# The next pair's value projection ahead of the last pair's final context group: a changed TensorE order in a two-layer attention kernel

## What is computed

```
q, k, v = tanh(x @ Wq + bq), tanh(x @ Wk + bk), tanh(x @ Wv + bv)     # per head: 1024 x 64
alpha   = softmax(causal(q @ k^T / sqrt(64)))
ctx     = alpha @ v
return tanh(ctx @ Wo + bo)
```

## Time and profile before

| | |
|---|---|
| median of 3 executions | 1946.13 us (1944.18 to 1951.32) |
| the profiled execution, its own time | 1945.94 us |
| its span in the trace | 1944.2 us |
| TensorE matmul busy | 1750.4 us, 90% |
| VectorE busy | 1436.0 us, 74% |
| ScalarE busy | 1376.0 us, 71% |
| GpSimd busy | 362.4 us, 19% |
| mean granted TensorE clock | 0.964 |

### The profile page before, as it was taken

One profiled execution on the slowest core, in us unless ns is written; L12 is line 12 of the kernel. 1 busy time (PEld: TensorE's weight loads), 2 busy tenths in 40 slices (PEclk: granted clock), 3 DMA queues, 4 the chain that ended last, 5 costly groups with the idle time before them and its releaser, 6 DMA issues. The chain is left out here.

```text
span 1944.2 us, 38151 instructions
## 1 busy us (share of the span) xinstructions
PE 1750.4 (90%) x12846; PEld 767.9 (39%) x12933; DVE 1436.0 (74%) x2573; ACT 1376.0 (71%) x1943; POOL 362.4 (19%) x349
## 2 busy tenths in 40 slices
PE   2899999999999999654999999999999999989995
PEld 2344444444444444330233333333333333256774
DVE  4477777888778888887677777777777777548888
ACT  4666666666666666352888888888888888855776
POOL 4111113333333333365200000000000000020004
PEclk8999999999999999866999999999999999989998
DMA  4101000000111000058011110111000100000001
GB/s 124 50 34 36 34 34 35 34 34 34 38 40 38 34 34 3 4 120 187 1 19 20 20 19 18 18 18 18 18 18 18 18 18 19 1 13 7 17 11 43
DMA packets 44966, 63.24 MB, mean 33 GB/s; under 512 B 7554, under 2 KB 32802, under 8 KB 43172
## 3 DMA queue, kind: packets, MB, share of 16 engines
q1 hardware_dynamic: 43856, 60.62, 11.6%
q10 hardware_dynamic: 1044, 1.76, 0.2%
HBM read 20.94 MB, written 13.11 MB: 18 GB/s over the span
## 5 line engine op out<-in xcount | busy, mean ns | idle before, releaser
L1348 ACT ACTIVATE arena<-psum 128x512 f32<-128x512 f32 x1024 | 556.3, 609 | 115.1 <-PE psum L1423 90.4
L630 ACT ACTIVATE arena<-psum 128x2048 f32<-128x2048 f32 (+1 forms) x160 | 273.3, 1708 | 231.6 <-PE psum L515 228.9
L1446 PE MATMUL psum<-arena 128*128 128x512 bf16 x983 | 302.4, 388 | 47.6 <-DVE arena L1054 22.2
L1054 DVE TENSOR_REDUCE arena<-psum 128x1 f32<-128x1024 f32 x256 | 309.7, 1210 | 28.8 <-PE psum L1446 27.7
L1049 DVE CUSTOM_DVE_ANT_0 arena<-psum,arena 128x512 f32<-128x512 f32 x256 | 177.0, 691 | 170.8 <-ACT arena L1340 170.1
L1423 PE MATMUL psum<-arena 128*128 128x512 bf16 x978 | 291.0, 382 | 10.1 <-ACT arena L1348 7.5
L532 PE MATMUL psum<-arena,hs 128*64 128x512 f32 (+3 forms) x1536 | 283.0, 496 | 2.7 <-POOL arena L679 2.2
L679 POOL TENSOR_SCALAR_AFFINE_SELECT arena<-arena 128x512 f32<-128x512 f32 (+1 forms) x160 | 168.9, 1073 | 563.5 <-ACT arena L630 563.5
L1436 PE MATMUL psum<-arena 128*32 128x512 f32 x2048 | 272.8, 605 | 0.7 <-ACT arena L1348 0.7
L515 PE MATMUL psum<-arena 64*128 64x512 f16 (+3 forms) x2304 | 215.4, 325 | 4.9 <-DVE arena L714 3.6
L1423 PEld LDWEIGHTS psum<-arena 128*128 128x128 bf16 x1024 | 98.4, 97 | 269.2 <-ACT arena L1348 193.9
(11 more groups left out here) (194 smaller groups left out, 2377.2 us busy)
## 6 DMA issues: line engine op xcount, KB each, us to landing
arena<-arena SPq DMA_DIRECT2D x32, 512.0 KB, 3.0
arena<-arena SPq DMA_DIRECT2D x48, 128.0 KB, 2.2
latent_k<-arena SPq DMA_DIRECT2D x12, 384.0 KB, 5.0
latent_kpm<-arena SPq DMA_DIRECT2D x12, 384.0 KB, 5.2
arena<-latent_q SPq DMA_DIRECT2D x48, 96.0 KB
arena<-latent_kpm SPq DMA_DIRECT2D x16, 288.0 KB
arena<-latent_k SPq DMA_DIRECT2D x16, 288.0 KB
arena<-arena SPq DMA_DIRECT2D x32, 96.0 KB, 2.6
```

Source lines behind the costliest of these rows:

```text
L630: nc.scalar.activation(probs[g], SC[:, :, 0:WIDTH[g]], ACT.Exp, scale=DH ** -0.5).then_inc(exp_done, 1)
L1054: nc.vector.tensor_reduce(tops[:, m:m + 1], slot, AX.X, ALU.max).then_inc(top_done, 1)
L1348: nc.scalar.activation(e_probs[u % 2][:, j, :], TS[(GH * u + j) % 3], ACT.Exp, scale=KD ** -0.5).then_inc(e_done, 1)
L1446: last = nc.tensor.matmul(slot[:, h * HALF:(h + 1) * HALF], q_rows[par][:, j, qt * P:(qt + 1) * P], k[:, j, h * HALF:(h + 1) * HALF], star ...
```

## The change

On TensorE alone, in each pair, the value projection of the next pair now stands ahead of the final context group of the last pair. Nothing else differs: the same instructions, the same waits, the same buffers.

```diff
@@ -563,10 +563,10 @@
                 def pair(i, par, last=False, norm=False):
+                    if not last:
+                        values(i + 1, 1 - par)
                     if at_least(i, 1):
                         context(i - 1, 4, 1 - par)
-                    if not last:
-                        values(i + 1, 1 - par)
                     scores(i, 1, par)
                     if not last:
                         project(i + 1, 0, 1 - par)
```

## The result

The changed kernel takes 2020.23 us (median of 4 executions, 1997.05 to 2026.54) against 1946.26 for the kernel before on the same chip, 74 us more. The recorded ratio is 1.0354, with a 95% interval of 1.027 to 1.0439; it isn't the quotient of the two medians, which is 1.038. I had forecast 1995 and a range that ended at 2003. The direction was right, the size was not: 74 us instead of 49.

What follows compares the result with a forecast made beforehand. A ring of waits through TensorE, ScalarE and VectorE bounds norm pairs; TensorE bounds plain pairs. Norm 38.2, plain 9.2, the turn between 0.8 and pairs 1 and 2 1.6 make 49.8 us more: 1995, range 1985 to 2003.

Steps and rivals of the forecast that it cites:

- Term 1: Values still wait for add_output: TensorE idles 2.2 us instead of 1.1 in norm pairs, 0.55 in plain pairs.
- Terms 2 to 4: Late context group delays its followers: value_tanh starts at V + 3.92, project 0 at V + 5.09, scores 2 at V + 8.36.
- V: Start of the value projection on TensorE, 0.15 us after add_output ends; the zero point for the forecast's times.
- second hole: New TensorE idle time ahead of project 0, waiting for value_tanh: 0.8 us.
- Term 5: ScalarE's chain from value_tanh to exp 2: exp 2 starts at V + 9.97 in norm pairs, before at V + 8.06.
- Term 6: VectorE follows exp 2 rigidly, so the delay reaches add_output; no slack counted, late round_ctx absorbed by idle times.
- The plain pairs: Pairs 1 to 9: 1.32 us more a turn from pair 3 on, 9.2 in all; pairs 1 and 2 0.8 each.
- The sum at full clock: All turn costs of the first attention added, without any clock drop: 49.8 us more.
- Rivals 1 and 2: Values' wait not a true one, 1948 us, 4%; only TensorE's order counts, 1972 us, 7%.
- A rule weighed: the clock: Norm pairs' idle times of 2.2 and 0.8 us might lower TensorE's clock; judged by busy share, left out of the sum.
- third rival: TensorE's clock falls in norm pairs: 1.7 us a pair, 34 us on top, 2030 us; 6%.
- the ring: Cycle of waits: values, ScalarE's tanh and exp steps, VectorE's sums and add_output, next values; norm turn 23.90 to 25.81 us.

Runs made afterwards that it cites:

- r2: Changed kernel with the scores of group 0 made twice in norm pairs, filling the hole ahead of the values: 1993.62 us, ratio 1.0237.
- r9: Changed kernel with value_tanh ahead of copy_out on ScalarE and the scores of group 0 made twice in norm pairs: 1992.27 us, ratio 1.0231.
- r3: Changed kernel with the first half of the final context group kept ahead of the values, only the second half behind: 1981.80 us, ratio 1.0172.
- r1: The changed kernel measured once more, nothing altered: 2012.15 us (1996.44 to 2024.63), ratio 1.0353.
- r4: Changed kernel with value_tanh ahead of copy_out on ScalarE: 2023.96 us, ratio 1.0394.
- r7: Changed kernel with VectorE's add_output moved earlier, directly behind spread: 1953.58 us, ratio 1.0032.
- r8: Kernel before the change with VectorE's add_output moved earlier, directly behind spread: 1926.79 us, ratio 0.9898.
- r10: Kernel before the change with the scores of group 0 made twice in norm pairs: 1950.18 us, ratio 1.0018.

## Why the prediction was wrong

**Right, by their terms.**
- *Term 1, the values' wait*: 35.1 / 17 = 2.06 us in norm pairs (forecast 2.2), released by add_output.
- *Terms 2 to 4*: V + 4.01, 5.09 and 8.36 in r2, against 3.92, 5.09 and 8.36. The second hole is 0.71 (0.8).
- *Term 5*: exp 2 at V + 9.87, 0.1 earlier than I took it, and r9 showed that ScalarE's chain does bind, as the term said. Norm turns grew by 25.67 - 23.90 = 1.77 (1.91).
- *Term 6*: VectorE gave back nothing. Its L714 idle times are still ended by L609; the late round_ctx shows as a new wait at L750 (57.6 us in 17 turns, the clock's share included) in front of those idle times, as expected.
- *The plain pairs*: 24.01 a turn (24.05), and pairs 1 and 2 together 124.28 - 122.76 = 1.5 (1.6). The one turn from plain to norm came out longer than forecast: 318.63 - 292.34 = 26.29 us (25.81).
- *The sum at full clock*: r2 is 1993.62 - 1947.32 = 46.3 us above the kernel before on its chip, forecast 49.8. The terms held to 3.5 us of 50; 20 norm turns at 1.77 instead of 1.91 are 2.8 of them.
- *Rivals 1 and 2*: both fell. V did not move to the end of scores 0, and the second hole was there.

One slip without effect: I spoke of 8 matmuls in the context group. The program issues 4, in fp32, and the trace records 8; the sum went by the rows' times.

**The step that failed** is the paragraph "A rule weighed: the clock" and the 6% it led to. I compared the busy share of a 5 us window, 3.17 of 5 at full clock in the first of the earlier trace rows, with the share that the changed place would have, found them alike, and kept the clock out of the sum. But the idle time in that window was in two pieces, 1.04 and 0.79 us, while the change makes one of 2.1. The share did come out as I took it (0.00 + 0.34 + 1.00 + 1.00 + 1.00 = 3.34 us of the 5 from 400 to 405), and the clock fell there all the same. The row that was nearer, the 5 us with idle times of 1.68 and 2.23 us after which the clock fell to a mean of 0.66, I set aside because its busy share was so much lower. And the trace before held single idle times of just the size in question, which I didn't look up. At two of 2.13 us, which end at 1716.67 and 1740.28, the clock fell, at one of 2.21 it didn't. The last two:

```profile
51.59 1.47 PE L480 MATMUL psum<-arena 128*128 128x512 f16 x6 [2.21 <-ACT arena L609]
...
52.00:53.00 1.00, 1.00 (x5) 0.29 (x3) 0.92 (x1) 0.00 (x0) 0.00 (x0) 1.00 0.00 0
...
1740.28 4.44 PE L1736 MATMUL psum<-arena 128*128 128x512 f16 x12 [2.13 <-ACT arena L1828]
...
1741.00:1742.00 1.00, 1.00 (x4) 0.42 (x3) 0.46 (x1) 1.00 (x2) 0.00 (x0) 0.50 0.03 8
```

By these rows a drop was anything but a remote case. Measured: the clock fell at most holes of 2.06 us in one execution (15 of 18 turns), at 4 in another, and at none of those of 1.5 (r3), 1.09 (before) or 0.67 (r2). The mechanism, its place and its price were on record as the third rival, 1.7 us a turn and 2030 in all; measured were 1.6 us a long turn (27.27 - 25.67) and up to 2027. Its chance was wrong, and so was the sign that I named for it, a granted clock below 0.95 between 100 and 800 us: the mean there was 0.96 in the profiled execution and 0.99 in r1, since the plain pairs and the short turns are averaged in. The Trainium skill, "TensorE: Matmul & The Clock Gate", section "A second HAM failure mode: psum-queue depth-cycling", tells of a kernel whose short idle times between groups of matmuls made the clock swing between its two levels. The trace agrees in that the granted clock went from 1.00 to 0.50 and back in 15 of 18 turns.

What stays open is which of these holes lets the clock fall, and so why the number of drops differs so much between executions of one program: 1996 and 2025 us came from the same kernel on the same chip, with holes of the same 1.98 and 2.11 us. In one profiled execution the long turns came 14 in a row, in r1 singly, and r4 had the drop in every turn of its profiled execution.

## What to carry to other kernels

When an instruction waits for another engine, what stands ahead of it in its queue is free up to the length of the wait. Moved behind, it costs its full length if the ring goes through it, and the reads that hang on it in another engine's queue come on top: here 1.02 us for the context group and 0.92 for copy_out were forecast, and a norm turn grew by 1.77. To win time at such a place, move the releaser (add_output: 1% off), not the work that fills the wait. And when two things are moved, compare kernels that differ in one: the new order costs 6.5 us against the kernel before (r7) but 26.8 against its true partner (r8).

When a change opens a hole on TensorE, price it twice, once as the wait and once as half clock for the matmuls behind it. Judge the second by looking up single idle times of the same length in the trace and the clock behind each, not by the busy share of a window; where they differ, as those of 2.13 and 2.21 us here, both outcomes belong in the forecast with weight. The longest idle time that the trace shows at full clock is no safe bound: behind the 2.21 us the clock held, behind most of those of 1.98 in the first profile after the change it fell. And if a kernel's executions scatter more than those of its neighbour, look at the granted clock first.

## What the runs showed of the hardware

- In the turn shown the drop came after the hole, not in it: TensorE was idle from about 399.7 to 401.66 at a granted clock of 1.00, ran again from 401.66, and only then fell to 0.50 and came back at about 406. In r1, at the hole of 2.42 us that ends at 319.69, it fell within the hole, some 0.4 us before its end.
- Useless matmuls in a hole of 2.06 us made the kernel 0.9% faster (2012.15 to 1993.62 on one chip). Its turns are those of the changed kernel at full clock (25.67 in both), so what it wins is the long turns.
- An added 1.41 us a pair cost only 24.10 - 23.90 = 0.20 us a turn in the kernel before (r10), since most of it went into the hole ahead of the values (18.8 / 18 = 1.04 us on average); where the last 0.17 us went isn't shown.
